# Squares of every second key sent by eight transfers a head, whole heads turned by TensorE at both ends, norm 2's scaling and the bias moved, the gate behind projections

## The reference

```python
x = _layernorm(x + _L0_attn_ref(x, L0_attn_W), axis=-1)
x = _layernorm(x + _L0_xattn_ref(x, ctx_1024, ctx_1024, ...), axis=-1)
x = _layernorm(x + _L0_ffn_ref(x, L0_ffn_cond, ...), axis=-1)

def _L0_xattn_ref(Q, K, V, Wq, bq, Wk, bk, Wv, bv, Wo, bo):
    ...
    q = (Q @ Wq + bq).reshape(b, len_q, H, DIM_K).transpose(0, 2, 1, 3)
    k = (K @ Wk + bk).reshape(b, K.shape[1], H, DIM_K).transpose(0, 2, 1, 3)
    v = (V @ Wv + bv).reshape(b, V.shape[1], H, DIM_V).transpose(0, 2, 1, 3)
    scale = 1.0 / np.sqrt(b).astype(np.float32)
    att = jnp.einsum('bhqd,bhkd->bhqk', q * scale, k)
    att = jax.nn.softmax(att, axis=-1)
    out = jnp.einsum('bhqk,bhkd->bhqd', att, v)
    out = out.transpose(0, 2, 1, 3).reshape(b, len_q, H * DIM_V)
    return out @ Wo + bo
```

## Time and profile before

| | us |
|---|---|
| median of 3 runs | 1884.77 (1883.41 to 1888.46) |
| profiled execution, its own time | 1884.64 |
| its span, first to last instruction | 1882.7 |
| TensorE busy | 1851.0 (98%) |
| VectorE busy | 1573.8 (84%) |
| ScalarE busy | 1160.6 (62%) |
| GpSimd busy | 1041.9 (55%) |
| mean granted clock of TensorE | 0.996 |

### The profile page before, as it was taken

How to read it: one execution, slowest core, us unless ns; L and a number is a source line. 1 busy time by engine, 2 the same in 40 slices (tenths; PEclk the granted TensorE clock), 3 DMA queues, 4 the chain that set the end, 5 groups by cost and what they waited for, 6 DMA issues and landing times.

```text
span 1882.7 us, 28845 instructions
## 1 busy us (share of the span) xinstructions
PE 1851.0 (98%) x8863; PEld 1528.0 (81%) x8863; DVE 1573.8 (84%) x3386; ACT 1160.6 (62%) x2461; POOL 1041.9 (55%) x1108
## 2 busy tenths in 40 slices
PE   9999999989999999999999999999999999999998
PEld 8888888768888888888888888888888877678887
DVE  6676666789898998999889898998989999858887
ACT  5444555567777676777767777777777766622221
POOL 2322234146567775665666565565666666736773
PEclk9999999999999999999999999999999999999999
DMA  5777787875858777585785957667486776412121
GB/s 224 274 290 278 282 305 277 319 251 184 262 167 299 227 248 231 150 268 168 236 268 165 303 151 254 209 194 238 147 267 208 229 235 197 142 67 86 59 81 67
DMA packets 200920, 400.39 MB, mean 213 GB/s; under 512 B 18112, under 2 KB 82112, under 8 KB 198592
## 3 DMA queue, kind: packets, MB, share of 16 engines
q1 hardware_dynamic: 164720, 329.08, 53.2%
q10 hardware_dynamic: 36048, 69.48, 11.2%
HBM read 211.31 MB, written 88.08 MB: 159 GB/s over the span
## 4 chain that ended last, share of the span: by engine, by line
PE 89%; DVE 6%; POOL 2%; DMA 2%; ACT 1%; issue 1%; ACTq 0%; POOLq 0%; DVEq 0%
PE a_proj L1407 17%; PE a_turned L1407 16%; PE a_av L1446 11%; PE a_score L1420 11%; PE a_proj L48 9%; PE a_proj L1832 5%; PE a_av L1832 5%; PE a_score L48 3%; PE a_av L48 3%; PE a_turned L1430 3%; PE a_proj L1430 2%; DVE all_negmax L1224 1%; DVE c_squares L1280 1%; DMA all_second_buffer<-x1T_scratch 1%; PE a_score L1807 1%
## 5 line engine op out<-in xcount | busy, mean ns | idle before, releaser
L1010 POOL TENSOR_SCALAR c_prob<-c_prob,all_rden 128x512 f32<-128x512 f32 x512 | 351.9, 695 | 498.4 <-DVE all_rden L1230 498.3
L1090 ACT ACTIVATE c_prob<-a_score,all_negmax 128x512 f32<-128x512 f32 x512 | 347.7, 684 | 196.6 <-DVE all_negmax L1224 193.5
L1224 DVE TENSOR_REDUCE all_negmax<-a_score 128x1 f32<-128x512 f32 x512 | 328.9, 684 | 97.4 <-PE a_score L1420 97.3
L1017 POOL TENSOR_TENSOR c_landing<-c_landing,c_flip_hi 128x512 fp32r<-128x512 f32 x250 | 317.8, 1292 | 4.0 <-ACT c_flip_hi L1140 4.0
L1280 DVE STREAM_TRANSPOSE c_squares<-c_prob 128x256 f32<-128x256 f32 x500 | 291.8, 622 | 3.3 <-POOL c_prob L1010 3.1
L1420 PE MATMUL a_score<-c_ks,c_qs 128*128 128x512 f32 x1024 | 278.2, 393 | 9.5 <-ACT c_prob L1090 9.4
L1420 PEld LDWEIGHTS a_score<-c_ks,c_qs 128*128 128x128 f32 x1024 | 190.6, 188 | 55.1 <-issue 9.4
L1446 PE MATMUL a_av<-c_pt,c_vs 128*128 128x512 f32 x512 | 159.4, 393 | 0.0
L343 POOL TENSOR_SCALAR s_prob<-s_prob,s_rden 128x512 f32<-128x512 f32 x32 | 22.2, 693 | 228.3 <-DVE s_rden L515 228.3
L1140 ACT CAST c_flip_hi<-c_landing 128x512 fp32r<-128x512 f32 x250 | 143.3, 625 | 1.7 <-issue 1.6
L1407 PE MATMUL a_proj<-all_third_buffer,all_first_buffer 128*128 128x512 f32 x564 | 141.8, 400 | 0.6 <-DVE c_ks L1249 0.6
(11 more groups left out here) (230 smaller groups left out, 4023.3 us busy)
## 6 DMA issues: line engine op xcount, KB each, us to landing
c_landing<-c_squares SPq DMA_DIRECT2D x500, 128.0 KB, 2.7
c_wk<-wk_scratch SPq DMA_DIRECT2D x64, 512.0 KB, 3.7
c_wq<-wq_scratch SPq DMA_DIRECT2D x64, 512.0 KB, 4.6
c_ks<-c_ks SPq DMA_DIRECT2D x128, 256.0 KB, 3.6
all_first_buffer<-ctxT_scratch ACTq DMA_DIRECT2D x60, 512.0 KB, 8.1
all_second_buffer<-x1T_scratch ACTq DMA_DIRECT2D x60, 512.0 KB, 6.9
ctxT_scratch<-s_csp SPq DMA_DIRECT2D x8, 2048.0 KB, 7.4
c_y<-y_steps_scratch SPq DMA_DIRECT2D x16, 1024.0 KB, 5.6
```

The source lines that it names most:

```text
L1010: nc.gpsimd.tensor_scalar(prob[:, n % 2, i, :], prob[:, n % 2, i, :], rden[:, n % 2, i:i + 1], 1.0, ALU.mult, ALU.mult).then_inc(p_ready, 1)
L1017: nc.gpsimd.tensor_tensor(whole, as_f32(whole), by_square(as_f32(flip_hi_part[:, k, :])), ALU.subtract).then_inc(flip_lo, 1)
L1090: nc.scalar.activation(prob[:, n % 2, i, :], spsum[:, i % 2, :], ACT.Exp, bias=negmax[:, n % 2, i:i + 1], scale=1.0, accum_out=den[:, n % ...
L1224: nc.vector.tensor_reduce(negmax[:, n % 2, i:i + 1], spsum[:, i % 2, :], AX.X, ALU.max, negate=True).then_inc(smax, 1)
```

## The change

- `squares_out` has another layout, and a VectorE transpose reads every second key (the key is 128k + 64m + 2j + e, with 32 values of j in a square) instead of every fourth. `landing` is filled with eight DMAs a head, each from 32 partitions to 64, of 64 KB, where there were four of 128 KB to all 128.
- `WHOLE` is heads 0 to 4 and 124 to 127, nine in place of three. Six more heads have 2 more turns each (12 turns of 4 transposes), with ScalarE's and VectorE's casts and subtractions; they have no transposes, sends or splits of squares. 119 flipped heads remain, with 476 transposes and 952 DMAs, for 500 and 500.
- The four L120 operations of norm 2's scaling go from group 14 (steps 12, 13, 13, 15) to group 15 (steps 5, 9, 11, 13), behind the step's subtractions.
- GpSimd builds the gate matrix in step 9 of group 15 instead of 10, and adds the first biases after its last `split_out` instead of in steps 9, 11, 13 and 14, without the wait for `av_mm`.
- In TensorE's epilogue each of the last two values comes before three quarters of an O item; the gate follows, then the last quarters.

```diff
--- before.py
+++ after.py
@@ -804,7 +805,8 @@
         return (g, T * head + k) if head >= 0 else (g - 1, T * (head + HH) + k) if g else None
 
 
-    WHOLE = (0, 1, HH * GROUPS - 1)
+
+    WHOLE = tuple(range(5)) + tuple(range(HH * GROUPS - 4, HH * GROUPS))
     FLIPS = {head: n + 1 for n, head in enumerate(h for h in range(HH * GROUPS) if h not in WHOLE)}
     LANDINGS = {head: sum(h % 2 == head % 2 for h in FLIPS if h <= head) for head in FLIPS}
 
@@ -848,13 +850,13 @@
     sp, pool, act, dve, pe = nc.sync, nc.gpsimd, nc.scalar, nc.vector, nc.tensor
     WV, cp, xp = held.third, held.first, held.second
     y, osum = sc.sb("y", [P, T, D]), sc.sb("osum", [P, 2, S])
-    squares_out = [sc.sb("squares0", [P, SQUARES, FLIPPED, T, Q])]
+    squares_out = [sc.sb("squares0", [P, 2, 2, FLIPPED, T * Q])]
     ks, qs = sc.sb("ks", [P, 2, 2, 2, S], F32R), sc.sb("qs", [P, 2, 2, S], F32R)
     pt, landing = sc.sb("pt", [P, TURNED, 2, S], F32R), sc.sb("landing", [P, 2, SQUARES, FLIPPED, T * Q], F32R)
     vs = sc.sb("vs", [P, 2, T, HH, 2 * DK], F32R)
     wk, wq = sc.sb("wk", [P, 2, K, P], F32R), sc.sb("wq", [P, 2, K, P], F32R)
     op, WO = sc.sb("op", [P, 2, PAIRS, S], F32R), sc.sb("WO", [P, 2, PAIRS, D], F32R)
-    squares_out.append(sc.sb("squares1", [P, SQUARES, FLIPPED, T, Q]))
+    squares_out.append(sc.sb("squares1", [P, 2, 2, FLIPPED, T * Q]))
     prob = sc.sb("prob", [P, 2, T, S])
     flip_hi_part = sc.sb("flip_hi", [P, FLIPPED, S], F32R)
     negmax, den, rden = held.softmax
@@ -922,9 +924,10 @@
         sp.wait_ge(flipped, T * FLIPS[head])
         wait(sp, av_mm, T * (head - 1))
         for a in range(SQUARES):
-            sp.dma_start(as_f32(landing[:, head % 2, a, :, :]).rearrange("p k n -> p (k n)"),
-                         squares_out[head % 2][a * Q:(a + 1) * Q].rearrange("p m k i q -> p (m k i q)")).then_inc(
-                             landed[head % 2], 16)
+            for m in range(2):
+                sp.dma_start(as_f32(landing[m * P // 2:(m + 1) * P // 2, head % 2, a, :, :]).rearrange("p k n -> p (k n)"),
+                             squares_out[head % 2][a * Q:(a + 1) * Q, m].rearrange("p e k n -> p (e k n)")).then_inc(
+                                 landed[head % 2], 16)
 
     def sync_weights():
         load_pair(wk, wkparts, 0, wk_loaded)
@@ -1054,17 +1057,13 @@
                 me.after.pool_split(WEIGHT_GROUPS.index(g), step - 7)
             if g == WEIGHT_GROUPS[0] and step == 6:
                 me.after.pool_clear()
-            if g == GROUPS - 1 and step == 10:
+            if g == GROUPS - 1 and step == 9:
                 pool.wait_ge(proj_mm, made("K", g, 3))
                 me.after.pool_gate()
             if g >= GROUPS - 2 and step < T:
                 if step == 0:
                     pool.wait_ge(held.bo_loaded, 16)
                 add_bo(nc, held, g - GROUPS + 2, 0, [step])
-            if g == GROUPS - 1 and step in (9, 11, 13, 14):
-                if step == 9:
-                    pool.wait_ge(av_mm, TILES * g)
-                me.after.pool_first_bias((9, 11, 13, 14).index(step))
 
     def gpsimd_all():
         for t in range(LEAD):
@@ -1073,6 +1072,8 @@
             pool_group(g)
         for j in (PAIRS - 2, PAIRS - 1):
             split_out(GROUPS - 1, j)
+        for i in range(T):
+            me.after.pool_first_bias(i)
 
     me.gpsimd_all = gpsimd_all
 
@@ -1135,7 +1136,7 @@
 
     def flip_hi_tile(g, n, k):
         head = HH * g + n
-        act.wait_ge(landed[head % 2], 16 * SQUARES * LANDINGS[head])
+        act.wait_ge(landed[head % 2], 32 * SQUARES * LANDINGS[head])
         wait(act, av_mm, T * (head - 1) + TURNED + k + 1)
         nc.scalar.copy(by_square(flip_hi_part[:, k, :]), as_f32(landing[:, head % 2, :, k, :])).then_inc(flip_hi, 1)
 
@@ -1276,10 +1277,10 @@
         head = HH * g + n
         dve.wait_ge(p_ready, TILES * g + t + 1)
         if i == 0:
-            wait(dve, landed[head % 2], 16 * SQUARES * (LANDINGS[head] - 1))
-        nc.vector.transpose(squares_out[head % 2][:, :, :, i, :].rearrange("p m k q -> p k m q"),
-                            prob[:, n % 2, i, TURNED * P:].rearrange("p (k j m) -> p k m j", k=FLIPPED, m=SQUARES)).then_inc(
-                                flipped, 1)
+            wait(dve, landed[head % 2], 32 * SQUARES * (LANDINGS[head] - 1))
+        nc.vector.transpose(
+            squares_out[head % 2][:, :, :, :, i * Q:(i + 1) * Q].rearrange("p m e k q -> p k m e q"),
+            prob[:, n % 2, i, TURNED * P:].rearrange("p (k m j e) -> p k m e j", m=2, j=Q, e=2)).then_inc(flipped, 1)
 
     def o_second(g, n):
         head = HH * g + n
@@ -1295,7 +1296,9 @@
             norm2.variance(nc, 0)
         if step == 12:
             norm2.inverse(nc, 0)
-        norm2.scale(nc, x2, x2, {12: [0], 13: [1, 2], 15: [3]}.get(step, []))
+
+    def norm_last(step):
+        held.norm2.scale(nc, held.x2[:, 0, :, :], held.x2[:, 0, :, :], {5: [0], 9: [1], 11: [2], 13: [3]}.get(step, []))
 
     def vector_group(g):
         last = g == GROUPS - 1
@@ -1322,6 +1325,8 @@
                 pt_lo_tile(*tile)
             if g == GROUPS - 2:
                 norm_first(step)
+            if last:
+                norm_last(step)
             if last and step == STEPS - 2:
                 me.after.turn_lo(0, 0, (0, 1), first_bank)
 
@@ -1488,12 +1493,11 @@
             tensor_group(g)
         for t in range(TILES - T - FLIPPED, TILES - FLIPPED):
             values(GROUPS - 1, t)
+        for item, t in zip(EPILOGUE[:2], range(TILES - FLIPPED, TILES)):
+            values(GROUPS - 1, t)
+            project(item, range(K - 1))
         pe.wait_ge(p_exp, TILES * GROUPS)
         me.after.gate(0, 0)
-        for t in range(TILES - FLIPPED, TILES):
-            values(GROUPS - 1, t)
-        for item in EPILOGUE[:2]:
-            project(item, range(K - 1))
         for item in EPILOGUE[:2]:
             project(item, [K - 1])
         me.after.turn_logits(0)
```

## The result

The changed kernel takes **1915.97 us** (median of 4 runs, 1911.71 to 1922.89), the kernel before 1885.73 beside it: a ratio of 1.0167, 95% interval 1.0147 to 1.0187. The forecast was 1888.6 with a range up to 1903: the sign of the small loss was right, the size was not, and the time lies outside the range.

The account below looks back on a forecast made before the run. TensorE, 98% busy, was taken as the bound, so only its waits in the end groups could change. Terms +7.2 - 3.2 + 3.6 - 3 - 1, plus 0.4 for its clock, on 1884.64 gave 1888.6 us, range 1875 to 1903.

Parts of the forecast that it names:

- the sign of the small loss: Whole kernel: +4.0 us on the profiled run's 1884.64, so slightly slower, 1888.6 us.
- What bounds the kernel: Steady cross-attention: TensorE is always busy, 10.03 us a head; freeing VectorE, ScalarE or GpSimd shortens nothing there.
- Squares read at every second key: VectorE transposes, four a head: 330 to 420 ns for 622; reaches TensorE's waits in groups 0, 14, 15 only, -1 us.
- Eight transfers a head: Sends on SP where the next batch's inputs load: last leaves 2.5 us later, squares' lateness covered; 0, up to +3.
- rival 2: Squares late in the load stretch, about 1 us in each of 14 groups: 1902.6 us, slower; chance 0.13.
- Whole heads: Groups 0 and 15: casts wait for single buffers and delay scores, in group 0 also loads; +7.2 and +3.6 us.
- Norm 2 and the gate: Scaling leaves group 14, -3.2 us, and costs 0 in group 15; gate behind projections in the epilogue, -3 us.
- the squares' -1: Groups 0, 14 and 15: quicker transposes shorten TensorE's waits for reciprocals and GpSimd's scaling, -1 us (-2 to 0).

Follow-up runs that it names:

- eight_wide: Kernel before with each of its four sends a head cut in two by key chunk, each landing in all 128 partitions: 1893.54 us, ratio 1.0056.
- ks_first: Changed kernel with the two copies of K issued before a head's eight sends in steps 6 and 14, instead of behind them: 1902.57 us, ratio 1.0092.
- eight_half: Kernel before, old transposes, each of four sends cut in two by source partitions, 64 KB from 16 partitions to 64: 1916.96 us, ratio 1.0177.
- eight_dot: Kernel before plus four extra sends a head, each of 128 bytes from one partition, to a tile nothing reads: 1898.16 us, ratio 1.0068.
- no_squares: The change without its squares part: old transposes and four sends, but nine whole heads, norm 2, bias and gate moved: 1888.0 us, ratio 1.002.
- moves_only: Kernel before with only norm 2's scaling, the bias, the gate matrix and the gate moved; squares and whole heads as before: 1877.66 us, ratio 0.9962.

## Why the prediction was wrong, and where it was right

**What bounds the kernel.** Right: outside the steps that wait for loads the distances of the middle groups are what they were, and VectorE's 86 us less of work changed none of them.

**Squares read at every second key.** Right: 418 ns, at the upper end of 330 to 420. The page "SBUF — State Buffer" of the Trainium skill ("Door 1: The DMA port swizzle") would have two hits a line reach the full rate; the trace shows the direction, 622 to 418 ns, but whether 418 is the full rate no run shows: half of the contiguous 690 ns row would be 345, and that row is a subtraction, not a transpose. Its -1 could not be seen by itself.

**Eight transfers a head: the step that failed.** It was costed at 0 and measured 28 us; rival 2 had it at one us a group, for the wrong reason. The sentence "SP has nothing else that is urgent in that place" is the error. SP has `double_k` and the load of wq behind the sends, and 2.5 us of delay on them were not followed on to what they then collide with. I had also measured the room of the squares at their landing and of nothing else in that stretch. In the changed kernel the squares do come as late as rival 2 has it: ScalarE waits for them in one head of most middle groups, 16 times and 11.4 us in all. But TensorE's wait at step 12 is not for them (in `eight_wide` ScalarE waits 49.1 us for squares and the kernel loses 9.6); it is for the x loads, whose room I had not priced in the middle groups at all. In the kernel before it was small: in one group the last chunk, issued at 734.7, landed 8.6 us later, at 743.3, and Q0+ began at 743.87.

```profile
L165 ACTq DMA_DIRECT2D all_second_buffer<-x1T_scratch x2: 526/580/635, 734.2 to 734.7; - x2
...
DMA to landing us min/median/max: 6.0/7.3/8.6
...
743.87 2.32 PE L1407 MATMUL a_turned<-all_second_buffer,c_wq 128*128 128x512 f32 x9
```

The loads' median landing went from 6.9 to 9.4 us, which eats that room and leaves one to two us in each of 13 groups. So the size of rival 2 (14 us) was half of what came (28), and its mechanism another. What stood behind the sends in SP's queue accounts for 13.4 of the 28, by `ks_first`; the cause of the other 14.6 stays open. The form of the sends, which the prediction left unpriced as well, has a part in it, by `eight_half` against `eight_wide`.
The Trainium skill had a rule that bears on it and that I didn't use: "DMA: Bandwidth & Descriptors", "Rules for kernel authors", says that two transfers to disjoint halves of the partitions share the same engines, so that one transfer to all 128 is to be preferred. `eight_half` (1916.96 against 1885.08) agrees with the advice, as far as it goes: by `eight_dot` (1898.16 against 1884.46), 13.7 of its 31.9 us come with four more issues of any size.

**Whole heads.** Right in mechanism. The sum, 10.8 us forecast and 10.3 measured by the medians (9.1 between the profiled executions), is right in part by luck: the two places are off against each other. Group 0 of the changed kernel, scores of steps 7 and 9 and Q0+, which answer:

```profile
379.48 0.59 ACT L1135 CAST c_pt<-a_turned 128x512 fp32r<-128x512 f32 x1 [2.71 <-PE a_av L1451]
...
398.15 1.40 PE L1425 MATMUL a_score<-c_ks,c_qs 128*128 128x512 f32 x4 [1.35 <-ACT c_prob L1091]
...
409.31 1.40 PE L1425 MATMUL a_score<-c_ks,c_qs 128*128 128x512 f32 x4 [1.68 <-ACT c_prob L1091]
...
425.30 3.01 PE L1412 MATMUL a_proj<-all_second_buffer,c_wq 128*128 128x512 f32 x12 [0.93 <-DMA all_second_buffer<-x1T_scratch]
```

Step 7 starts at 398.15 (forecast 400.2), Q0+ at 425.30 (429). The loads were mis-sized: the x chunks landed after 4.5 to 6.4 us, without squares in their way, and I had taken over 8. `no_squares` is 4.1 us behind `moves_only` at the start of group 1, for 7.2 forecast. In group 15 it loses 4.7 for 3.6: both steps came at 4.48 us, as by the earlier trace rows, but the last turns wait too (1.25 us for GpSimd's scaling). Of the changed kernel:

```profile
1649.12 1.07 PE L1425 MATMUL a_score<-c_ks,c_qs 128*128 128x512 f32 x4
...
1653.60 1.48 PE L1425 MATMUL a_score<-c_ks,c_qs 128*128 128x512 f32 x4 [2.08 <-ACT c_prob L1091]
...
1677.71 0.33 PE L1435 MATMUL a_turned<-all_ident,c_prob 128*128 128x128 f32 x1 [1.25 <-POOL c_prob L1013]
```

**Norm 2 and the gate.** Right. The three scores of the earlier trace rows now stand 10.60 us apart for 14.00, which is -3.4 for -3.2:

```profile
1589.34 1.07 PE L1425 MATMUL a_score<-c_ks,c_qs 128*128 128x512 f32 x4
...
1594.22 1.31 PE L1425 MATMUL a_score<-c_ks,c_qs 128*128 128x512 f32 x4 [0.16 <-ACT c_prob L1091]
...
1599.94 1.07 PE L1425 MATMUL a_score<-c_ks,c_qs 128*128 128x512 f32 x4
```

From the last scores to the turn of the logits it was 26.6 us (1640.88 to 1667.45) and is 22.6 (1671.96 to 1694.54), -4.0 for -3: the 2.66 us of the earlier trace rows are gone, and nothing waits in front of the gate.

```profile
1671.96 1.07 PE L1425 MATMUL a_score<-c_ks,c_qs 128*128 128x512 f32 x4
...
1691.23 1.97 PE L1811 MATMUL a_score<-f_x2T_even,f_G 128*128 128x512 f32 x8
...
1694.54 0.60 PE L1819 MATMUL a_score<-all_ident,f_logitT 128*128 128x128 f32 x4
```

All terms but the squares' -1 sum to 1889.6 us, and `no_squares` ran in 1888.0: +2.9 on the kernel beside it for +5.0. That is close partly because group 0, 3.1 us over, is set against group 15, 1.1 under.

## What to carry to other kernels

When a queue gets more to issue, a good part of the price can lie not in what it sends but in what stands behind it (here 13.4 of 28 us): list the queue's next entries, move each by the added time, and ask which other transfers they then meet. Where DMA is busy for a whole stretch, each load in it needs its own margin, from landing to first use, measured before the change; a compute engine at 100% before tells only that no margin is used up yet. Turning more work on the bound engine costs its instructions and also the single buffers behind them: here a whole head cost its neighbours' waits, not its own 0.7 us.

## What the runs showed of the hardware

- DMA engines that are busy all the time (share 1.04 to 1.06) moved 288 GB/s in one order of issues and 355 in another, in the same stretch of two kernels that differ in that order alone (267 and 349 over 13 groups); what changed is that two 256 KB copies between partitions went ahead of the sends. What in those copies slows the rest was not tried by itself.
- An extra send of 128 bytes takes as long to issue as one of 64 or 128 KB, about 0.6 us of SP, and four of them a head cost 13.7 us in all (`eight_dot`).
- A transpose on VectorE that reads every second float32 takes 418 ns for 256 elements a row, for 622 with every fourth.
- Eight sends of 64 KB to one half of the partitions each cost some 22 us more (`eight_half`, 1916.96 against 1885.08) than eight to all 128 (`eight_wide`, 1893.54 against 1883.99), with the same bytes. This is not explained.
